# Experts of a two-layer network: from masked products over all tokens to tokens sorted by expert on the chip, 23 tiles with one expert each

## The reference

```python
x = L0_attn_x                                   # (1, 2048, 128)
xn = _layernorm(x); s = _L0_attn_ref(xn, ...); g = _silu(_L0_ffn_ref(xn, ...)); x = x + s * g
xn = _layernorm(x); s = _L1_attn_ref(xn, ...); g = _silu(_L1_ffn_ref(xn, ...)); x = x + s * g

def _L1_ffn_ref(x, Wr, br, ln_g, ln_b, W1, b1, W2, b2):     # D, F, E = 128, 512, 8
    router_probs = softmax(xt @ Wr + br)
    gates, idx = max(router_probs), argmax(router_probs)
    onehot = one_hot(idx, E)
    xn = (xt - mu) * rsqrt(var + LN_EPS) * ln_g + ln_b
    h = relu(einsum('te,td,edf->tf', onehot, xn, W1) + b1[idx])
    y = einsum('te,tf,efd->td', onehot, h, W2) + b2[idx]
    return y * gates
```

## Time and profile before

| | |
|---|---|
| median of 3 runs | 3418.86 us (3417.58 to 3419.49) |
| the profiled execution's own time | 3421.26 us |
| its span, first to last instruction | 3419.4 us |
| busy on PE, POOL, DVE, ACT | 92%, 70%, 69%, 42% of the span |
| mean granted PE clock | 0.952 of full speed |
| router block, from 1482.2 us | 28.5 us |
| second normalisation, from 1510.7 us | 21.1 us |
| expert products, from 1531.8 us | 360.5 us |
| projections of layer 1, from 1892.3 us | 158.2 us |
| attention of layer 1 to the end, from 2050.5 us | 1368.9 us |

### The profile page before, as it was taken

How to read it: one execution, slowest core, us unless ns; L and a number is a source line. 1 busy time by engine, 2 the same in 40 slices (tenths; PEclk the granted TensorE clock), 3 DMA queues, 4 the chain that set the end, 5 groups by cost and what they waited for, 6 DMA issues and landing times. The chain is left out here.

```text
span 3419.4 us, 47107 instructions
## 1 busy us (share of the span) xinstructions
PE 3133.3 (92%) x18389; PEld 1247.1 (36%) x18389; DVE 2356.3 (69%) x3610; ACT 1427.8 (42%) x1609; POOL 2394.8 (70%) x1080
## 2 busy tenths in 40 slices
PE   5949999999999999948888985999999999999997
PEld 3414444444444444333333431333333333333333
DVE  6545555555555555351211696999999999999996
ACT  3325555555555555510000222555554555545544
POOL 0019999999999999900000383888888888888887
PEclk9969999999999999958888997999999999999998
DMA  3341111112111111010000133111111111112200
GB/s 80 126 123 26 25 26 26 26 26 49 26 26 26 26 26 25 1 51 0 0 0 0 49 148 97 49 49 49 49 49 49 49 49 49 49 54 60 60 23 13
DMA packets 53617, 148.69 MB, mean 43 GB/s; under 512 B 17155, under 2 KB 24076, under 8 KB 51220
## 3 DMA queue, kind: packets, MB, share of 16 engines
q1 hardware_dynamic: 53396, 145.67, 15.5%
HBM read 110.78 MB, written 34.87 MB: 43 GB/s over the span
## 5 line engine op out<-in xcount | busy, mean ns | idle before, releaser
L847 POOL TENSOR_TENSOR a_total<-a_total,room 128x1024 f32<-128x1024 f32 x768 | 1815.3, 2364 | 141.9 <-ACT room L740 37.3
L650 PE MATMUL a_ov<-room,va 128*64 128x512 f32 x4096 | 991.6, 605 | 0.0
L774 DVE TENSOR_REDUCE a_mx<-a_jb 128x1 f32<-128x1024 f32 x512 | 627.2, 1225 | 508.6 <-PE a_jb L613 508.6
L733 ACT ACTIVATE room<-room,sscale 128x1024 f32<-128x1024 f32 x512 | 588.4, 1149 | 650.5 <-DVE room L794 650.4
L740 ACT ACTIVATE room<-a_st,sscale 128x1024 f32<-128x1024 f32 x512 | 548.8, 1111 | 556.6 <-PE a_st L639 556.6
L769 DVE CUSTOM_DVE_ANT_0 a_junk<-a_jb,a_tab 128x1024 bf16<-128x1024 f32 x512 | 623.8, 1218 | 50.9 <-PE a_jb L613 34.6
L794 DVE TENSOR_TENSOR room<-a_st,a_tab 128x1024 f32<-128x1024 f32 x512 | 623.7, 1219 | 5.2 <-PE a_st L639 3.0
L612 PE MATMUL a_jb<-a_kh,a_qh 64*128 64x512 f16 x1024 | 396.6, 387 | 102.0 <-DMA a_tab<-bias_line 30.9
L847 POOL TENSOR_TENSOR a_total<-room 128x1024 f32<-128x1024 f32 x128 | 302.5, 2363 | 182.4 <-ACT room L733 135.6
L639 PE MATMUL a_st<-a_qh,a_kh 64*128 64x512 f16 x2048 | 394.9, 382 | 21.0 <-DVE room L794 21.0
L650 PEld LDWEIGHTS a_ov<-room,va 128*64 128x64 f32 x4096 | 248.4, 136 | 423.6 <-issue 363.7
(11 more groups left out here) (181 smaller groups left out, 2616.1 us busy)
## 6 DMA issues: line engine op xcount, KB each, us to landing
a_tab<-bias_line SPq DMA_DIRECT2D x16, 1984.0 KB, 12.1
qk_high<-q_oh SPq DMA_DIRECT2D x32, 512.0 KB, 2.6
qk_low<-q_ol SPq DMA_DIRECT2D x32, 512.0 KB, 3.6
a_qh<-qk_high SPq DMA_DIRECT2D x64, 256.0 KB, 4.9
a_kh<-qk_high SPq DMA_DIRECT2D x64, 256.0 KB, 5.7
a_ql<-qk_low SPq DMA_DIRECT2D x64, 256.0 KB, 6.3
a_kl<-qk_low SPq DMA_DIRECT2D x64, 256.0 KB, 6.7
ex_w<-in_L_ffn_W SPq DMA_DIRECT2D x1, 2048.0 KB, 10.5
```

What stands on the lines that cost most here:

```text
L650: last = nc.tensor.matmul(ov[t * DH:(t + 1) * DH, :], k.va[:, 2 * s + t, h * DH:(h + 1) * DH], prob[:, step % RING, t * QC:(t + 1) * QC], ...
L733: nc.scalar.activation(prob[:, r, :], prob[:, r, :], ACT.Exp, scale=k.sscale[:, layer:layer + 1])\
L774: nc.vector.reduce_max(mx[:, j // 2, j % 2:j % 2 + 1], jb[:, :], AX.X).then_inc(max_done, 1)
L847: nc.gpsimd.tensor_tensor(t, first, prob[:, step % RING, :], ALU.add).then_inc(summed, 1)
```

## The change

The three blocks of the experts become two, and work goes to the two neighbours of layer 0 and layer 1:

- `route_stage` normalises and routes in one block. The rank of a token among those of its expert comes from a product with a triangle of ones (`tri`) and from running sums over the 16 tiles (`before`); each expert gets whole tiles of 128 rows, so the place `spot` of each token in a list of 23 x 128 rows is known. `tiles` holds the expert of each of the 23 tiles, `hot` the same as a one-hot matrix. POOL scatters the normalised tiles with 16 indirect transfers into `sorted_in` in HBM.
- `expert_tiles_stage` loads the sorted tiles, turns them, and multiplies each by the weights of one expert alone. PE loads 23 expert numbers into registers first. The first weights are copied by POOL into `w1i`, with a register for the place; the second are addressed by PE with the register. The 23 tiles go back to `sorted_out`.
- In `qkv_stage` of layer 1, POOL gathers the 16 tiles of the gate with 16 indirect transfers ahead of its copy and its additions, and ACT makes silu at the end of the block.
- In `ternary_ffn_stage`, POOL writes a block of zeros and SP stores it over `sorted_in`, after its loads.

The loop over 23 tiles is written out, whatever the routing is. The core of the diff:

```diff
+TL = NT + NE - 1
@@ ternary_ffn_stage
+            sp.wait_ge(blanked, 1)
+            sp.dma_start(k.sorted_in.rearrange("(i p) d -> p i d", p=P),
+                         blank[:, :].unsqueeze(1).broadcast_to([P, TL, D])).then_inc(cleared, 16)
+            sp.wait_ge(cleared, 16)
@@ qkv_stage
+            if rotate:
+                act.wait_ge(gathered, 16 * NT)
+                for q in range(NT):
+                    nc.scalar.activation(k.gate[:, q, :], k.gate[:, q, :], ACT.Silu, scale=k.prob[:, q:q + 1])
         @block.gpsimd
         def _(pool):
             if rotate:
+                for q in range(NT):
+                    nc.gpsimd.indirect_dma_start(k.gate[:, q, :], None, k.sorted_out[:, :],
+                                                 bass.IndirectOffsetOnAxis(ap=k.spot[:, q:q + 1], axis=0))\
+                      .then_inc(gathered, 16)
                 nc.gpsimd.tensor_copy(flat(k.wo[:, :, :]), flat(k.wo1[:, :, :]))
@@ route_stage, POOL
+            pool.wait_ge(placed, 1)
+            for q in range(NT):
+                pool.wait_ge(tile_done, q + 1)
+                nc.gpsimd.indirect_dma_start(k.sorted_in[:, :], bass.IndirectOffsetOnAxis(ap=k.spot[:, q:q + 1], axis=0),
+                                             k.acc[:, q, :], None).then_inc(scattered, 16)
@@ route_stage, PE
             for q in range(NT):
-                nc.tensor.matmul(ps[:, q, :], k.xnT[:, q * P:(q + 1) * P], wr[:, :], start=(q == 0), stop=False,
-                                 skip_group_check=True)
-                last = nc.tensor.matmul(ps[:, q, :], k.ones[0:1, 0:P], br[:, :], start=False, stop=True,
-                                        skip_group_check=True)
+                last = nc.tensor.matmul(ps[:, q, :], k.xnT[:, q * P:(q + 1) * P], wr[:, :], start=True, stop=True)
             last.then_inc(made, 1)
+            pe.wait_ge(counted, 6)
+            pe.wait_ge(added, 1)
+            nc.tensor.matmul(tot[:, :], k.ones[:, :], before[:, 0, 2 * NT - 1, :], start=True, stop=True)
+            nc.tensor.matmul(flat(pos[:, :, :]), tri[:, :], flat(onehot[:, :, :]), start=True, stop=False)
+            nc.tensor.matmul(flat(pos[:, :, :]), k.ones[:, :], flat(before[:, 0, NT - 1:2 * NT - 1, :]),
+                             start=False, stop=True).then_inc(ranked, 1)
@@ route_stage, DVE (after onehot)
+            for i, back in enumerate((1, 2, 4, 8)):
...
+                link(nc.vector.tensor_tensor(dst[:, NT:2 * NT, :], src[:, NT:2 * NT, :],
+                                             src[:, NT - back:2 * NT - back, :], ALU.add))
...
+            link(nc.vector.scalar_tensor_tensor(logit[:, :, :], first, float(P), pos[:, :, :], ALU.mult, ALU.add))
+            link(nc.vector.tensor_tensor(logit[:, :, :], logit[:, :, :], onehot[:, :, :], ALU.mult))
+            link(nc.vector.tensor_reduce(spot[:, :], logit[:, :, :], AX.X, ALU.add))
+            nc.vector.tensor_copy(k.spot[:, :], spot[:, :]).then_inc(placed, 1)
+            for q in range(NT):
+                nc.vector.tensor_scalar(k.acc[:, q, :], k.xn[:, q, :], mv[:, q, 0:1], rstd[:, q:q + 1],
+                                        ALU.subtract, ALU.mult).then_inc(scaled, 1)
...
+                nc.vector.tensor_tensor(k.acc[:, q, :], k.acc[:, q, :], gain[:, :], ALU.mult).then_inc(scaled, 1)
...
+                nc.vector.tensor_tensor(k.acc[:, q, :], k.acc[:, q, :], shift[:, :], ALU.add).then_inc(tile_done, 1)
@@ expert_tiles_stage, SP
+            sp.wait_ge(scattered, 16 * NT)
+            for g in range(NG):
+                a, b = 4 * g, members(g)[-1] + 1
+                sp.dma_start(xs[:, a:b, :], k.sorted_in[a * P:b * P, :].rearrange("(i p) d -> p i d", p=P))\
+                  .then_inc(xs_loaded, 16)
...
+            for g in range(NG):
+                a, b = 4 * g, members(g)[-1] + 1
+                sp.wait_ge(y_copied, g + 1)
+                sp.dma_start(k.sorted_out[a * P:b * P, :].rearrange("(i p) d -> p i d", p=P), ys[:, a:b, :])\
+                  .then_inc(fetched, 16)
+            sp.wait_ge(fetched, 16 * NG)
@@ expert_tiles_stage, PE
+            owners = [pe.value_load(tiles[0:1, i:i + 1], min_val=0, max_val=NE - 1) for i in range(TL)]
...
+            def upward(i):
+                if i % 4 == 0:
+                    pe.wait_ge(xs_copied, i // 4 + 1)
+                pe.wait_ge(w1_picked, i + 1)
+                if i >= 2:
+                    pe.wait_ge(relu_act, i - 1)
+                    pe.wait_ge(relu_dve, i - 1)
+                for j in range(FT):
+                    last = nc.tensor.matmul(up[:, i % 2, j // 2, (j % 2) * P:(j % 2 + 1) * P], w1i[:, i % 2, j * P:(j + 1) * P], xsT[:, i, :],
+                                            start=True, stop=True)
+                last.then_inc(up_done, 1)
+            def downward(i):
+                g = i // 4
+                o = dn[:, g % 2, i % 4, :]
...
+                nc.tensor.matmul(o, hot[:, i:i + 1].broadcast_to([NE, P]), b2[:, :], start=True, stop=False)
+                pe.wait_ge(relu_act, i + 1)
+                pe.wait_ge(relu_dve, i + 1)
+                for j in range(FT):
+                    w = w2[:, j, bass.ds(owners[i], 1), :].rearrange("p a d -> p (a d)")
+                    last = nc.tensor.matmul(o, hT[:, i % 2, j, :], w, start=False, stop=(j == FT - 1))
+                last.then_inc(dn_done, 1)
+            turn(0)
             pe.wait_ge(weights_loaded, 16 * (1 + FT))
+            for i in range(TL):
+                if i % 4 == 0 and i // 4 + 1 < NG:
+                    turn(i // 4 + 1)
+                upward(i)
+                if i >= 1:
+                    downward(i - 1)
+            downward(TL - 1)
@@ expert_tiles_stage, POOL
+            for i in range(TL):
+                owner = pool.value_load(tiles[0:1, i:i + 1], min_val=0, max_val=NE - 1)
+                if i >= 2:
+                    pool.wait_ge(up_done, i - 1)
+                nc.gpsimd.tensor_copy(w1i[:, i % 2, :], w1[:, bass.ds(owner, 1), :].rearrange("p a f -> p (a f)"))                  .then_inc(w1_picked, 1)
```

More of the change, by code:

```diff
@@ new lines, in _ @@
+            for i, back in enumerate((1, 2, 4)):
+                src, dst = ends[:, i % 2, :], ends[:, (i + 1) % 2, :]
+                link(nc.vector.tensor_tensor(dst[:, NE:2 * NE], src[:, NE:2 * NE], src[:, NE - back:2 * NE - back],
+                                             ALU.add))
+            first = ends[:, 1, NE - 1:2 * NE - 1].unsqueeze(1).broadcast_to([P, NT, NE])
+            link(nc.vector.scalar_tensor_tensor(logit[:, :, :], first, float(P), pos[:, :, :], ALU.mult, ALU.add))
@@ new lines, in _ @@
+            last = ends[:, 1, NE:2 * NE].unsqueeze(1).broadcast_to([P, TL, NE])
+            link(nc.vector.tensor_tensor(reached[:, :, :], count[:, :].unsqueeze(2).broadcast_to([P, TL, NE]), last,
+                                         ALU.is_ge))
+            link(nc.vector.tensor_reduce(owner[:, :], reached[:, :, :], AX.X, ALU.add))
+            link(nc.vector.tensor_scalar(owner[:, :], owner[:, :], NE - 1.0, None, ALU.min))
+            link(nc.vector.tensor_copy(tiles[:, :], owner[:, :]))
@@ L985, in expert_products_stage, with expert_tiles_stage @@
[L985 removed]
+def expert_tiles_stage(nc, k, t, tiles, hot, w1, w2, scattered, weights_loaded, fetched):
     with ExitStack() as ctx:
@@ new lines, in _, with turn @@
+            pe.wait_ge(loaded, 32)
+            for j in range(FT):
+                last = nc.tensor.matmul(bt[:, j, :], b1[:, j * P:(j + 1) * P], hot[:, :], start=True, stop=True)
+            last.then_inc(spread, 1)
+            owners = [pe.value_load(tiles[0:1, i:i + 1], min_val=0, max_val=NE - 1) for i in range(TL)]
+            def turn(g):
+                if g % 2 == 0:
+                    pe.wait_ge(xs_loaded, 16 * min(g + 2, NG))
+                if g >= 2:
+                    pe.wait_ge(xs_copied, g - 1)
+                for i in members(g):
+                    last = nc.tensor.transpose(tp[:, g % 2, i % 4, :], xs[:, i, :], k.ident[:, :])
+                last.then_inc(turned, 1)
@@ new lines, in _, with copy_x @@
+        @block.scalar
+        def _(act):
+            act.wait_ge(spread, 1)
+            nc.scalar.activation(b1t[:, :, :], bt[:, :, :], ACT.Copy).then_inc(b1_copied, 1)
+            act.wait_ge(b1_copied, 1)
+            def copy_x(g):
+                act.wait_ge(turned, g + 1)
+                n = len(members(g))
+                nc.scalar.activation(xsT[:, 4 * g:4 * g + n, :], tp[:, g % 2, 0:n, :], ACT.Copy).then_inc(xs_copied, 1)
+            copy_x(0)
+            for i in range(TL):
+                if i % 4 == 0 and i // 4 + 1 < NG:
+                    copy_x(i // 4 + 1)
+                act.wait_ge(up_done, i + 1)
+                if i >= 2:
+                    act.wait_ge(dn_done, i - 1)
+                for j in range(2):
+                    last = nc.scalar.activation(hT[:, i % 2, j, :], up[:, i % 2, 0, j * P:(j + 1) * P], ACT.Relu,
```

(17 more changed lines are left out.)

256 lines of the change are left out of this document (119 added, 137 removed).

## The result

The changed kernel takes 3134.55 us (median of four runs, 3132.86 to 3136.29) where the kernel before, beside it, takes 3418.25 us (3417.58 to 3419.49). The ratio is 0.917 (95% interval 0.9154 to 0.9186). The forecast was 3164 with a range of 3132 to 3225. The change is 283.7 us where about 255 were forecast, so the time lies 29.5 us under the forecast and only 2.6 above the lower end of the range. The profiled execution took 3134.13 us.

The account below looks back on a forecast made before the run. Stages follow one another, so savings add; PE, partly waiting for DVE, sets the old expert block. Changes of -255.9 (expert blocks) and +0.8 (projections) take 3421.3 to 3166.2 us; the median, 2.4 lower, is about 3164, range 3132 to 3225.

Parts of the forecast that it names:

- Routing: Routing block: places known at 1501.3, 16 scatters at 1.27 us, POOL ends it 4.6 us behind DVE, at 1523.0.
- Closing the block costs 0.5: End of the routing block: 0.5 us from POOL's last scatter at 1522.5 to the block's end at 1523.0.
- The rival in which DVE holds POOL up: Routing block: DVE's work lengthens a scatter to 1.77 us, the block ends 8 us later, total 3172; chance 14%.
- Start of the tiles: Head of the expert block: PE loads 23 registers at 0.8 us, 18.4 us (3.5 to 44); first turn at 1545.1.
- The 23 tiles: Expert products on PE: records, register instructions and waits, and a slow start, together 87.5 us, to 1632.6.
- I take 0.1 for each of the nine, 0.9 a tile, 20.7 us: Tiles: four register instructions and about five waits per tile add 20.7 us (10 to 95) to PE's records.
- Together 62.8 us: PE's 19 records a tile over 23 tiles: upward 25.1, downward with bias 34.5, turns 3.2 us.
- about 4 us lost: Start of the tiles' products: PE at a granted clock of 0.50, a record 0.26 us instead of 0.14.
- The end of the block, the gathers and the silus: Last copy, store and close 3.8 us; layer 1 projections: gathers, 20.3 us, hidden in POOL's idle time, silus lose 0.8.
- registers and waits cost nearly nothing: Rival: register loads at 0.3 (-11.5), 0.05 a wait (-10.4), POOL under DVE's pace (-4.6): 3137 us; chance 9%.
- the case that was given 53%: The whole kernel goes as forecast, stage by stage: 3164 us; chance 53%.
- POOL's longest pass: Rival: indirect transfers take 3.27 us each, +32 in the routing and +17.1 before layer 1's additions: 3213; chance 12%.

Follow-up runs that it names:

- the last two runs: Changed kernel with the product with the second bias left out, then with that product added twice: 3123.0 and 3136.57 us.

## Why the prediction was right, and where its sizes were off

**What bounds the kernel: right.** The stages still follow one another. Attention of layer 1 is 1368.4 us, and the saving of the expert blocks reached the end in full.

**Routing: right to 1.7 us, and that is the closing.** The places are known at 1499.9 instead of 1501.3, but the first scatter follows 1.8 us behind them and not 0.9, so two small errors nearly cancel. The scatters' 1.26 us is nearly the price that was taken from POOL's short pass (1.27): the row behind it is of other work, an addition over 512 columns, so that it comes this close is luck. POOL ends the block behind DVE. What was mis-sized is "Closing the block costs 0.5": 2.2 us behind the last scatter, 0.5 where there is none. The rival in which DVE holds POOL up did not come: apart from the first one, two of the 16 scatters took longer than 0.96 us, 1.07 and 1.11. The Trainium skill, page "SBUF — State Buffer", section "Who interferes with whom", would have allowed a wait of up to 0.34 us behind every `tensor_scalar`. This trace shows at most 0.15 us in two scatters and, the other way round, at most 0.08 in a few of DVE's `tensor_scalar` of a tile and 0.21 in a small one over 23 columns (L1048: 0.39 us, 0.18 in the run without scatters).

**Start of the tiles: the mechanism right, 5.1 us too long.** PE is silent as predicted, and the run without the loads shows them as the cause and the sorted rows as what is late next. The 23 loads took 15.1 us and not 18.4 (0.66 each for 0.8), and the eight bias products, 2.1 us in the sum, lie beside them: the first load starts at 1526.1, and PE works off these products from 1526.12 to 1528.0. The Trainium skill, page "DMA: Bandwidth & Descriptors", section "Latency and other measured facts", has some 600 ns as the floor of such a load. The trace agrees if the step from one load to the next is meant, 0.66 us; the load's own row is 0.30 and that of its register instruction 0.15.

**The 23 tiles: this is the step that failed in size, 27.8 of the 32.0 us.** A tile takes 2.6 us (59.7 / 23), where PE was to be busy "at about 3.7 us a tile". Its three terms:
- "I take 0.1 for each of the nine, 0.9 a tile, 20.7 us": they cost nothing that the runs can show. Fixed addresses leave the pace as it is, PE has no idle time in 59.7 us, and even a whole load in each tile adds nothing. The bound from below was 10, so the term's range did not hold its value. What failed is the overlap: the term adds the sequencer's work to that of the array, by a hand-over between two engines that waited for each other. Here the sequencer runs ahead (its last register instruction of L1148 starts at 1599.6, the last product at 1601.0), so its work lies beside the products and no hand-over is on the path.
- "Together 62.8 us": 57.4, the 59.7 less the slow start of the next point. By the last two runs it is 437 records at 0.112 and 23 times 0.38 for the switch to the bias and back: 48.9 + 8.7 = 57.6, an estimate that agrees. The row of layer 0 is the same sum (ten records at 0.112 and 0.38 give its 1.50), so the downward part was priced right; the upward one, with no bias, was given 1.09 where eight records take 0.90, 4.4 us in all, and the turns 0.14 for 0.112.
- "about 4 us lost" at the low clock: about 2.3. The granted clock was 0.61 in the first 6 us and 1.00 in the 54 after them:

```profile
1541.00:1547.00 6.00, 5.71 (x28) 5.18 (x29) 1.17 (x4) 2.38 (x6) 1.05 (x2) 0.61 0.00 0
1547.00:1601.00 54.00, 54.00 (x410) 48.69 (x410) 16.30 (x48) 15.50 (x47) 11.89 (x20) 1.00 0.09 26
```

28 records took 6.0 us where at the later pace (54.0 / 410 = 0.132) they take 3.7. A wait of 0.30 us for ACT's first copy lies in the 2.3 as well.

**The end of the block, the gathers and the silus: right.** 3.4 us for 3.8; the gathers hidden, with the run that moves them as the proof; 0.65 us for 0.8 at the silus. Layer 0's zeros cost nothing that shows: the routing begins at 1481.8 for 1482.2, and it differs by more than that between executions.

**The rivals.** The one that came nearest in its result is "registers and waits cost nearly nothing" (3137, 9%), nearer than the case that was given 53%. It was right in its direction on the waits, to which it still gave 0.05 each, and wrong on the loads, which stayed at 0.66 and not 0.3; its 4.6 us at POOL did not come. So that it comes within 2.5 us is in part luck: it took too much off the loads and POOL and too little off the tiles. The indirect transfers were not at POOL's longest pass, and the clock did not stay low.

**Left open.** What the closing of a block does in its 2.2 us behind the last scatter; why the register loads took 4 us longer in one execution; what the 0.38 us around the 8-row product are.

## What to carry to other kernels

Price a register instruction or a wait by whether the sequencer can run ahead of its engine: among products that are already queued it cost nothing here, at the head of a block that has nothing queued it cost its full length. So it pays to load values from memory into registers one by one where they are used, or in a block where the engine is idle, and not all at the start (12 to 14 of 3134 us here). And a row of the profile that gives a group of records holds the switches at its ends as well: before it is used for another group, take a second row with another mixture and solve for both.

## What the runs showed of the hardware

- An indirect transfer of 128 rows of 512 bytes costs POOL 0.96 us as a scatter and 0.945 as a gather, and a gap of 0.30; the first of a row is longer (1.20 for the scatters, 1.51 to 1.81 for the gathers). It lands 2.2 to 2.5 us after its start in the median. DVE beside the scatters works at 0.93 us a tile, without them at 0.91.
- A load of a register by PE's sequencer is 0.30 us, with its register instruction (0.15) and gaps 0.66 from one to the next. Among products that are already queued it was hidden in full, one for each 2.4 us.
- A product whose weights' address comes from a register took the same time as one with a fixed address.
- At a granted clock of 1.00, f32 records of 128 x 128 come every 0.112 us; one change to a product with 8 rows and back costs 0.38 us on top, with one pair of records of 8 rows between or with two.
- A block that ends with POOL's indirect transfers took 2.2 us to close behind the last instruction of them in nine of ten kernels, and 0.5 where there were none.
